# A transformer layer on one core: image rows of 4 and 8 KB, batch 0 from SBUF to SBUF, fp32 products behind every second unit

## The reference

```
qkv    = x @ attn_w.T + attn_b                  # 16 heads of 8 features
scores = k @ q.T / sqrt(8), causal mask, softmax over the keys
x1     = layernorm(x + (probs @ v) @ out_w.T + out_b)
q8     = round(x1 / s_row) in int8, w8 = round(ffn_w / s_col) in int8
y      = layernorm(x1 + (q8 @ w8) * s_row * s_col)
```

## Time and profile before

| | before |
|---|---|
| median of 3 runs | 272.97 us (272.25 to 273.11) |
| profiled execution, own time | 272.08 us |
| profiled execution, span | 270.3 us |
| mean granted TensorE clock | 0.932 |
| busy: TensorE, weight loads, VectorE, ScalarE, GpSimd | 85, 65, 69, 68, 48% |
| DMA | 32.77 MB in 50,887 packets, mean 121 GB/s |

### The profile page before, as it was taken

One profiled execution on the slowest core, in us unless ns is written; L12 is line 12 of the kernel. 1 busy time (PEld: TensorE's weight loads), 2 busy tenths in 40 slices (PEclk: granted clock), 3 DMA queues, 4 the chain that ended last, 5 costly groups with the idle time before them and its releaser, 6 DMA issues.

```text
span 270.3 us, 8065 instructions
## 1 busy us (share of the span) xinstructions
PE 228.8 (85%) x2997; PEld 175.0 (65%) x2999; DVE 187.6 (69%) x529; ACT 185.0 (68%) x384; POOL 129.7 (48%) x255
## 2 busy tenths in 40 slices
PE   6361889999999999999999999999999999898710
PEld 3231666778787877787777787777777777665300
DVE  4702867676777888888787878787878878444631
ACT  3894135857686878787878787877777676888420
POOL 7514012314244564646464647474738424355664
PEclk9855679999999999999999999999999999999955
DMA  4397427764748347464747474848374701020001
GB/s 136 120 229 128 124 62 211 153 183 117 185 123 179 88 141 148 149 131 151 134 154 140 146 153 142 154 139 163 137 141 138 141 19 24 23 54 10 22 19 40
DMA packets 50887, 32.77 MB, mean 121 GB/s; under 512 B 7200, under 2 KB 50848, under 8 KB 50848
## 3 DMA queue, kind: packets, MB, share of 16 engines
q1 hardware_dynamic: 50704, 32.06, 48.5%
q10 hardware_dynamic: 144, 0.20, 0.3%
HBM read 17.17 MB, written 14.68 MB: 118 GB/s over the span
## 4 chain that ended last, share of the span: by engine, by line
PE 71%; ACT 10%; issue 5%; DVE 4%; POOL 4%; DMA 4%; SPq 1%; POOLq 0%; ACTq 0%; DVEq 0%
PE pv_bank L903 16%; PE dve_bank L866 15%; PE act_bank L866 12%; PE act_bank L924 5%; PE dve_bank L870 5%; PE act_bank L870 5%; PE act_bank L934 4%; ACT heads_t L525 3%; PE dve_bank L948 3%; PE dve_bank L966 3%; DMA k_stat<-imagek 2%; PE dve_bank L914 1%; DVE part_max L670 1%; PE act_bank L976 1%; ACT k_stat L565 1%
## 5 line engine op out<-in xcount | busy, mean ns | idle before, releaser
L487 ACT ACTIVATE probs<-act_bank 128x512 f32<-128x512 f32 x160 | 96.3, 603 | 44.5 <-PE act_bank L870 40.8
L670 DVE TRANSPOSE_TENSOR_REDUCE part_max<-dve_bank 128x16 f32<-128x512 f32 x160 | 110.3, 707 | 14.1 <-PE dve_bank L870 12.9
L866 PE MATMUL dve_bank<-q_move,k_stat 124*128 124x192 bf16 (+3 forms) x512 | 66.7, 246 | 10.2 <-DVE part_max L670 7.3
L866 PE MATMUL act_bank<-q_move,k_stat 128*128 128x192 bf16 (+3 forms) x512 | 61.5, 233 | 0.4 <-DMA q_move<-shift 0.4
L866 PEld LDWEIGHTS dve_bank<-q_move,k_stat 124*128 124x128 bf16 x512 | 40.5, 118 | 30.2 <-issue 11.2
L903 PE MATMUL pv_bank<-probs,v_stat 128*32 128x256 f32 (+3 forms) x1024 | 48.7, 305 | 9.1 <-ACT heads_t L525 9.1
L416 POOL TENSOR_TENSOR qk_rest<-qk_f,qk_parts 128x512 f32<-128x512 f32 x15 | 17.5, 1164 | 76.8 <-ACT qk_f L505 76.8
L866 PEld LDWEIGHTS act_bank<-q_move,k_stat 128*128 128x128 bf16 x512 | 43.2, 114 | 3.0 <-DMA q_move<-shift 0.8
L870 PE MATMUL dve_bank<-causal,identb 128*128 128x256 bf16 (+1 forms) x160 | 42.0, 263 | 0.0
L870 PE MATMUL act_bank<-causal,identb 128*128 128x256 bf16 (+1 forms) x160 | 40.2, 251 | 0.0
L903 PEld LDWEIGHTS pv_bank<-probs,v_stat 128*32 128x32 f32 x1024 | 23.9, 109 | 20.2 <-ACT heads_t L525 12.5
(11 more groups left out here) (92 smaller groups left out, 325.5 us busy)
## 6 DMA issues: line engine op xcount, KB each, us to landing
imageq<-qk_parts SPq DMA_DIRECT2D x32, 192.0 KB, 1.9
imagek<-qk_parts SPq DMA_DIRECT2D x32, 192.0 KB, 2.1
q_move<-imageq SPq DMA_DIRECT2D x32, 192.0 KB, 3.9
k_stat<-imagek SPq DMA_DIRECT2D x32, 192.0 KB, 4.3
xt_in<-xt_dram SPq DMA_DIRECT2D x16, 128.0 KB, 4.2
x_in<-x_dram SPq DMA_DIRECT2D x16, 128.0 KB, 3.3
out_dram<-o SPq DMA_DIRECT2D x16, 128.0 KB, 1.9
q_move<-shift SPq DMA_DIRECT2D x32, 8.0 KB
```

The costliest lines, as they stand in the source:

```text
L487: act.activation(probs[u][:, :], act_bank[at % ACT_BANKS][:, :], ACT.Exp, scale=SCALE).then_inc(act_emptied, 1)
L670: dve.tensor_reduce(out32, dve_bank[at % DVE_BANKS][:, :].rearrange("k (c q) -> k c q", q=32), op=ALU.max, axis=AX.X, apply_transpose=True ...
L866: pe.matmul(bank[:, at:at + TOK - blk * KB], keys, q_move[b % QK_RING][0:rows, p, blk * KB:TOK], start=(at == 0), stop=False, skip_group_c ...
```

## The change

- **Products.** The two heads of a pair now stand side by side in a block of 16 rows per product, so the six products take rows 0 to 95 in blocks of 16. `PRODUCTS` names the part of q and of k in each block. Weights and bias of q and k are re-ordered so that the projections come out in the order of the rows.
- **Images.** Each part is written once, as a plane: q as 16 rows of 4 KB, k as 16 rows of 8 KB, in which the half of the other head is zero. The zeros are put into all four k images once (`zero_image`). A batch is written in six DMAs and read in six, two products each: 32 rows of `q_move` or `k_stat` from two planes, or from one plane repeated.
- **Batch 0** goes from `qk_parts` to `q_move` and `k_stat` with eighteen DMAs from SBUF to SBUF, six on q from SyncE and twelve on k from SyncE and ScalarE. The fixed rows are set in buffer 0 and copied to buffers 1 to 3.
- **Emptying.** ScalarE empties q and k once, as fp32. GpSimd makes the first part as a cast.
- **Order.** The value groups are the five pairs of units. Fp32 products stand behind u = 1, 3, 5, 7 and 9. `LEAD` is 6. Output projection and first sum come at u = 9 of the phase of the heads, not at u = 0 of the next. The constants are set up in phase -1.

The diff, cut to its core:

```diff
-Q_PART = (1, 0, 0, 2, 1, 0)
-K_PART = (0, 0, 1, 0, 1, 2)
+PRODUCTS = ((0, 0), (2, 0), (0, 1), (0, 2), (1, 0), (1, 1))
+NPROD, ROWS = len(PRODUCTS), 2 * HD
+FIRST_LOADS, READS, WRITES = 3 * NPROD, NPROD, 2 * PARTS
+K_PLANE = ROWS * PAIRS * 2 * TOK
-LEAD = 8
+LEAD = 6
-PV_GROUPS = [(0, 1), (2, 3, 4), (5, 6), (7, 8, 9)]
+PV_GROUPS = [(u, u + 1) for u in range(0, NU, 2)]
...
+        def place_first(eng, product, heads):
+            q_part, k_part = PRODUCTS[product]
+            row = ROWS * product
+            if heads is None:
+                eng.dma_start(q_move[0][row:row + ROWS, :, :], qk_parts[0][:, q_part, 0, :]).then_inc(first_loaded, 16)
+                return
+            for s in heads:
+                eng.dma_start(k_stat[0][row + HD * s:row + HD * s + HD, :, s, :],
+                              qk_parts[0][64 * s:64 * s + 64, k_part, 1, :]).then_inc(first_loaded, 16)
...
-            def write_image(b, half):
...
-                for w in range(2):
-                    at = RUNS[w][half]
-                    sp.dma_start(image[w][b % QK_RING][:, 3 * half:3 * half + 3, :],
-                                 qk_parts[b % 2][:, at:at + 3, :]).then_inc(image_written[b % QK_RING], 16)
+            def write_image(b, n):
...
+                k = k_image[b % QK_RING][n * K_PLANE:(n + 1) * K_PLANE + 2 * TOK].rearrange("(s e) -> s e", s=2)
+                k = k[:, 0:K_PLANE // 2].rearrange("s (x q) -> s x q", q=2 * TOK)[:, :, 0:TOK]
+                sp.dma_start(q_image[b % QK_RING][n].rearrange("x (p q) -> (x p) q", p=PAIRS),
+                             qk_parts[b % 2][:, n, 0, :]).then_inc(image_written[b % QK_RING], 16)
+                sp.dma_start(k, qk_parts[b % 2][:, n, 1, :]).then_inc(image_written[b % QK_RING], 16)
+            def two_of(planes, parts):
+                a, b = parts
+                if a == b:
+                    return planes[a].unsqueeze(0).to_broadcast([2, ROWS, planes.shape[-1]])
+                return planes[a:b + 1:b - a]
...
-                for s in range(2):
-                    rows = slice(s * ROWS, (s + 1) * ROWS)
-                    q = image[0][slot].rearrange("(p s i) r q -> s (i r) p q", s=2, i=HD)
-                    k = image[1][slot].rearrange("(p s i) r q -> s (i r) p q", s=2, i=HD)
-                    sp.dma_start(q_move[slot][rows, :, :], q[s]).then_inc(qk_loaded[slot], 16)
-                    sp.dma_start(k_stat[slot][rows, :, s, :], k[s]).then_inc(qk_loaded[slot], 16)
+                k = k_image[slot][0:PARTS * K_PLANE].rearrange("(n x q) -> n x q", n=PARTS, x=ROWS)
+                for product in range(0, NPROD, 2):
+                    rows = slice(ROWS * product, ROWS * (product + 2))
+                    q_two, k_two = zip(*PRODUCTS[product:product + 2])
+                    sp.dma_start(q_move[slot][rows, :, :], two_of(q_image[slot], q_two)).then_inc(qk_loaded[slot], 16)
+                    sp.dma_start(k_stat[slot][rows, :, :, :], two_of(k, k_two)).then_inc(qk_loaded[slot], 16)
...
             def phase(b):          # SyncE
-                write_image(b + 3, 1)
+                write_image(b + 3, 2)
+                load_xt(b + 5)
                 read_image(b + 3)
...
                 load_x(b)
                 write_image(b + 4, 0)
+                write_image(b + 4, 1)
...
-                act.activation(first, src, ACT.Identity, bias=bias[:, w:w + 1])
-                act.activation(whole, src, ACT.Identity, bias=bias[:, w:w + 1]).then_inc(act_emptied, 1)
+                act.activation(dst, src, ACT.Identity, bias=bias[:, w:w + 1]).then_inc(act_emptied, 1)
...
             def phase(b):          # TensorE, behind the units
-                    if u == 0:
-                        project_out(b - 2)
-                        project_v(b + 1)
-                    if u == 1:
-                        turn_zq(b - 3)
-                    if u == 2:
-                        pv(b - 1, 3)
+                    if u == 1:
+                        pv(b - 1, 4)
+                        project_v(b + 1)
+                        turn_zq(b - 3)
+                    if u == 3:
+                        if b >= -1:
+                            project_qk(b + 4, 0)
+                        pv(b, 0)
                     if u == 4:
-                        pv(b, 0)
                         feed_forward(b - 3)
                     if u == 5:
+                        turn_pv(b - 1)
                         turn_maxima(b + 1)
-                        turn_pv(b - 1)
-                    if u == 6 and b >= -1:
-                        project_qk(b + 4, 0)
-                        project_qk(b + 4, 1)
+                        if b >= -1:
+                            project_qk(b + 4, 1)
+                        pv(b, 1)
                     if u == 7:
-                        pv(b, 1)
-                    if u == 8:
                         turn_heads(b - 1)
+                        pv(b, 2)
                     if u == 9:
-                        pv(b, 2)
+                        project_out(b - 1)
+                        pv(b, 3)
```

More of the change, by code:

```diff
@@ L47 @@
 PARTS = 3
-Q_PART = (1, 0, 0, 2, 1, 0)
-K_PART = (0, 0, 1, 0, 1, 2)
[L51 to L56, removed]
+PRODUCTS = ((0, 0), (2, 0), (0, 1), (0, 2), (1, 0), (1, 1))
+NPROD, ROWS = len(PRODUCTS), 2 * HD
+FIRST_LOADS, READS, WRITES = 3 * NPROD, NPROD, 2 * PARTS
+K_PLANE = ROWS * PAIRS * 2 * TOK
+LAST_ROW, SHIFT_ROW = NPROD * ROWS, 124
 DEPTH = SHIFT_ROW + 4
@@ L92 @@
 ACT_BANKS, DVE_BANKS = 4, 3
-ACT_EXTRAS = {0: [("v", 1)], 1: [("zq", -3)], 6: [("q", 4), ("k", 4)], 8: [("heads", -1)]}
-DVE_EXTRAS = {0: [("out", -2)], 4: [("ffn", -3)], 5: [("shift", 1), ("pv", -1)]}
+ACT_EXTRAS = {1: [("v", 1), ("zq", -3)], 3: [("q", 4)], 5: [("k", 4)], 7: [("heads", -1)]}
+DVE_EXTRAS = {4: [("ffn", -3)], 5: [("pv", -1), ("shift", 1)], 9: [("out", -1)]}
 def real(b):
@@ L172, in build_program @@
         qk_rest = sb("qk_rest", [128, 2, TOK])
[L173 to L176 removed]
+        qk_parts = [sb(f"qk_parts{i}", [128, PARTS, 2, TOK], BF16) for i in range(2)]
+        part = [[qk_parts[i][:, n, :, :] for n in range(PARTS)] for i in range(2)]
         q_move = [sb(f"q_move{i}", [128, PAIRS, TOK], BF16) for i in range(QK_RING)]
@@ L199, in build_program @@
         rstd = [sb(f"rstd{n}", [128, 3, TILES]) for n in range(2)]
-        image = [[nc.dram_tensor(f"image{w}{i}", (128, NPROD, TOK), BF16, kind="Internal").ap()
-                  for i in range(QK_RING)] for w in "qk"]
+        q_image = [nc.dram_tensor(f"q_image{i}", (PARTS, ROWS, PAIRS * TOK), BF16, kind="Internal").ap()
+                   for i in range(QK_RING)]
+        k_image = [nc.dram_tensor(f"k_image{i}", (PARTS * K_PLANE + 2 * TOK,), BF16, kind="Internal").ap()
+                   for i in range(QK_RING)]
         act_bank = [ps(f"act_bank{i}", [128, 512]) for i in range(ACT_BANKS)]
@@ L222, in build_program @@
         ones_loaded = sem("ones_loaded")
+        rows_copied = [sem(f"rows_copied{i}") for i in range(QK_RING)]
         x_loaded = [sem(f"x_loaded{i}") for i in range(RING)]
@@ L225, in build_program @@
         image_written = [sem(f"image_written{i}") for i in range(QK_RING)]
+        image_zeroed = [sem(f"image_zeroed{i}") for i in range(QK_RING)]
         qk_loaded = [sem(f"qk_loaded{i}") for i in range(QK_RING)]
@@ new lines, in place_first_queries @@
+            def place_first_queries():
+                sp.wait_ge(pool_setup, 1)
+                sp.wait_ge(q0_cast, 1)
+                for product in (0, 2, 3):
+                    place_first(sp, product, None)
+                wait_split(sp, 0, 3)
+                for product in (4, 5):
+                    place_first(sp, product, None)
+                wait_split(sp, 0, 4)
+                place_first(sp, 1, None)
+                sp.wait_ge(rows_set, 1)
+                place_first(sp, 3, range(2))
@@ L404, in _ @@
                                         base=-row, pattern=[[-1, 2], [0, TOK]], channel_multiplier=1))
-            step(pool.memset(k_stat[1][:, :, :, :].bitcast(F32), 0.0))
             assert done[0] == POOL_FIRST, done[0]
@@ L467, in phase @@
             def phase(b):
+                split(b + 3, True)
                 norm_factors(b - 2, 0, y_stats, rstd_made)
@@ L686, in second_part @@
                 if real(b):
-                    wait(dve, qk_split, b, 2)
-                    dve.tensor_copy(part[b % 2][1], qk_rest[:, :, :]).then_inc(qk_split[1], 1)
+                    wait_split(dve, b, 2)
+                    dve.tensor_copy(part[b % 2][1], qk_rest[:, :, :]).then_inc(split_of(b), 1)
             def make_shift(b, step):
```

228 lines of the change are left out of this document (139 added, 89 removed).

## The result

| | median, us | runs | ratio to before (95% interval) | span, us | clock |
|---|---|---|---|---|---|
| before | 273.04 | 272.25 to 273.23 | 1 | 270.3 | 0.932 |
| after | 472.96 | 472.41 to 474.3 | 1.730 (1.723 to 1.737) | 471.3 | 0.759 |
| predicted | 438 | range 380 to 585 | 1.604 | 434.8 | |

The chip has a slower state that some executions fall into; medians here are of all runs and ratios of those outside that state alone, which matters for e11, where two of four runs were slow and the ratio stands for 338 us.

A forecast was written before the change was run, and what follows sets the result against it. Two DMA engines, filled by narrow transfers, were to replace TensorE as the bound: 24.0 us of load plus 1.0 of gap, period 25. Start 20, fourteen periods to 370, reads landed at 387, plus 47.8: span 434.8, time 438 us, range 380 to 585.

The forecast's parts named there:

- rival 2: Image reads spread over 16 engines, 3.1 us a batch; TensorE stays the bound, 265 us (257 to 272); chance 0.13.
- 13.9 + 1.4 for the reads: Load per batch on the two busy engines: 13.9 us for q and repeated k reads, 1.4 for two plain k reads.
- 5.6 for the k writes: k image writes, 98,304 B in 512 B packets on each of two engines at 17.5 GB/s: 5.6 us a batch.
- 1.0 for a gap: Between a batch's last image write and the first byte read, transfers idle; 1.0 us added to the period.
- the way through TensorE: From a batch's shift load to its last write: 13.7 us of TensorE plus some 4 of transfer, 18, under 25.
- 20 +- 4: At the start, the reads of batch 1 are issued at 20 us, give or take 4, against 19.99 before.
- "4 + 5 us" of gain at the start: At the start, zeroings go and batch 0 skips DRAM: 4 + 5 us gained, setup in phase -1 taking back 1 to 2.
- The end: Batch 15's reads issued at 370, landed at 387 with TensorE at unit 4 of phase 13, then 47.8 us: span 434.8.
- Value groups and emptying: Value groups cost 0.5 to 0.6 us, an 0.56 wait goes: net 0 +- 0.3 a batch; emptying changes covered by TensorE.
- Rival 1: All six image reads run on two engines, unbroken planes of k included; 9.7 us a period more, 574 us; chance 0.17.
- the main case: Repeated or strided image reads on two engines, unbroken k planes on 16; period 25 us, time 438 us; chance 0.62.

The follow-up runs named there:

- e11: Twelve 16-row reads and six 64-row k writes as in e3, but ScalarE issues the shift load behind unit 6: 342.0 us, ratio 1.235 to the kernel before.
- e1: Changed kernel with its six reads of two planes split into twelve reads of one plane, 16 rows each: 364.95 us, ratio 1.335 to the kernel before.
- e4: Changed kernel with a hole of 512 elements between the planes of k, so neighbouring planes are not joined: 576.3 us, ratio 2.109 to the kernel before.
- e2: Changed kernel with each of the three k writes split into two writes of 64 rows: 460.81 us, ratio 1.686 to the kernel before.
- e12: Changed kernel with k read in three plain DMAs, q in six of 16 rows, shift and x loads ahead of the reads, k writes narrow: 287.45 us, ratio 1.051.
- e3: Changed kernel with twelve reads of 16 rows and six k writes of 64 rows: 354.59 us, ratio 1.297 to the kernel before.
- e9: Kernel of e3 with each product's rows spread six apart (n, n + 6, n + 12, ...) instead of 16 neighbouring: 341.43 us, ratio 1.245 to the kernel before.
- e10: Changed kernel, reads and writes still narrow, with the shift load issued by ScalarE behind unit 6 instead of by SyncE: 473.38 us, ratio 1.729.

## Why the prediction was right, and where its sizes were off

**The mechanism: right.** A transfer with an outermost dimension of 2 runs on two engines: 0.13 of the time of 16 in the trace, e1 takes it from the reads (-108 us), e4 adds it to two more (+103 us). Both have the 2 on the source side, which is what rival 2 had doubted. That neighbouring planes are joined to one wide transfer is what e4 undoes. Two engines moved 24 GB/s each, where 23.6 was taken.

**The period: 25 forecast, 26.0 measured, but not as a plain sum.** The prediction added the loads of the fullest engine: 13.9 + 1.4 for the reads, 5.6 for the k writes, 1.0 for a gap. The reads' 15.3 is as measured (15.3 from the shift load's issue to its landing). The k writes' 5.6 is not a term by itself: e2 took them out and won 0.5 a batch, where the sum without them would be 20. That a sum with a false term of 5 us came within 1 us of the period is luck. What stayed when the k writes were wide is chain 1, 10.9 us of TensorE and 15.3 of waiting behind the reads. The prediction had named this wait, and then priced the way through TensorE at 18 us (13.7 and 4 of transfer); with its own 15.3 in the place of the 4 that way comes to 29, above the 25, and would have had to be worked out closely. Chain 2, which it meant, has 3.7 us for the landing of the last write where it took 1.0. No run took the shift load out of its place behind narrow reads, so which of the two chains leads in a given batch stays open.

**The reads of batch 1: issued at 20 +- 4 by the forecast, at 25.8 measured.** The mis-sized term is the placing of batch 0. Its eighteen short DMAs were counted, but not whom they hold up. ScalarE after:

```profile
7.41 8.18 ACTq L303 DMA_DIRECT2D k_stat<-qk_parts  x10
15.64 1.06 ACT L641 ACTIVATE v_stat<-warm 128x1024 f32<-128x1024 f32 x1 [9.12 <-issue]
16.60 1.06 ACT L581 ACTIVATE qk_f<-act_bank,bias 128x256 f32<-128x256 f32 x2
```

Ten issues take 8.2 us of ScalarE, and q and k of batch 1 are emptied at 16.6 us behind them. Before, this stood at 9.8 us:

```profile
9.77 0.48 ACT L505 ACTIVATE qk_f<-act_bank,bias 128x256 f32<-128x256 f32 x1
```

This is 6.8 us later. The "4 + 5 us" of gain at the start did not come either: TensorE's first scores stand at 19.1 us, where they were at 18.3, and in the place of its wait of 6.03 us is one of 21.6 (next point). e12, whose reads are wide, still has its first exponential 8.8 us late. No run undid the placing alone.

**The first batches: no term in the prediction.** The copies of the fixed rows (L412, L413) stand behind the reads of batch 1: TensorE's longest wait in the trace is 21.6 us for `k_stat<-k_stat` and ends at 47.5, ahead of the first exponential (10.2 us at the same place in e12). Then phases 0 and 1 take 69.1 us (43.2 and 25.9), where two periods of 25 were meant. The chain shows what the shift load of batch 1 stands behind:

```profile
61.64 10.96 SPq L361
72.64 0.53 SPq L363
73.21 3.38 SPq L321
76.64 0.69 SPq L361
77.37 5.03 DMA k_image<-qk_parts
82.41 0.64 SPq L382
...
87.67 0.58 SPq L392
88.29 16.17 DMA q_move<-shift
```

A write held for 11 us behind the reads, the clearing of an image (L321), a write and its landing, then the reads of batch 3 and two more copies of fixed rows: 26 us of SyncE's list before the load is issued.

**The end: 64.8 forecast from the reads of batch 15 (434.8 less 370), 74.2 measured** (397.1 to 471.3). TensorE does not stand at unit 4 of phase 13 but at unit 0: the shift load of batch 13 is queued behind these reads.

```profile
400.44 0.41 SPq L383
...
401.55 15.16 DMA q_move<-shift
```

The three together: 5.8 at the start, 21.3 in 14 periods (371.3 for 350, the early ones up to 29.4) and 9.4 at the end are 36.5 us, the distance of the spans, 471.3 to 434.8.

**Value groups and emptying: right.** Net 0 +- 0.3 a batch was forecast; e12's 13.75 against 13.73 is the measurement of all these edits together.

**Rivals.** Rival 1 was worth asking (576 us in e4 beside its 574), though that its price was met is luck: the step from the main case was 103 and not 136 us, and the main case lay 35 us higher than forecast. Rival 2's price was wrong: with every transfer wide the kernel takes 355 us and not 265. Two of its steps failed. It moved the reads' 1.18 MB at 377 GB/s, the rate of a 128-row write, where 16 neighbouring rows get 120. And it priced SyncE by its image DMAs alone, 12 at 0.47 us, where the whole list has 17 issues in the changed kernel and 26 with wide transfers, and where the shift load, on which TensorE waits, stands behind twelve of them. What separates 355 from 287 (e3 to e12) is put down to these two and the order. One at a time, e9 took 13 us and e11 17; how the rest divides was not run one by one. The narrow k writes are still in e12 and its period is 13.75, so behind wide reads and in this order they hold no batch up.

## What to carry to other kernels

Count for each DMA the outermost dimension of both sides, and write a copy out of few planes as several plain ones or as one joined block: here an outermost 2 cost 108 us. Then look at what stands behind a slow transfer: a small load on the critical way waited out the reads ahead of it in its own queue, and on another queue it took turns with them packet by packet, which with packets of 64 B was no faster. Issue it first, as e12 does. And when large transfers become many small ones, add up the whole list of the issuing engine, at some 0.5 us each, before calling them hidden; the same holds for a compute engine that is made to issue.

## What the runs showed of the hardware

- Behind six reads, four of them on two engines, the issue itself stalls: two loads of 8 KB took SyncE 9.88 us, and 10.84 and 10.96 us were seen in the first batches.
- Sixteen neighbouring rows as destination: 120 GB/s with all 16 engines taken; the same 16 rows six partitions apart: 306 GB/s for a full share.
- An issue with spread rows took 0.59 us where one with neighbouring rows took 0.42 (e9 and e3).
- Within SyncE's queue the shift load's packets start after the last packet of the reads (205.9 and 205.7 us). On ScalarE's queue they take turns with them, one for one: 92 of 260 in 8 us in e10. It landed after 14.5 us all the same, and mostly after 6.5 to 7.1 in e11.
- A packet of 8 KB took 0.32 us on two engines, and on 16 engines 1.00 us into 16 neighbouring rows (e3) and 0.38 into 16 rows six apart (e9).
